# First attention of a two-layer network on one core: the loop over head pairs covers pairs 0 to 5, and the next batch's preparation sits at other places

## What is computed

```python
x = x + _L0_xattn_ref(_layernorm(x), ctx_768, w_q, w_kv, w_out, b_out)
# in it, per batch: 16 heads of 64 columns
q = query @ w_q;  k, v = jnp.split(context @ w_kv, 2, axis=-1)
scores = jnp.einsum('bhqd,bhkd->bhqk', q, k) * SCALE     # 512 x 1024 a head
attn = jax.nn.softmax(scores, axis=-1)
out = jnp.einsum('bhqk,bhkd->bhqd', attn, v)
return out @ w_out + b_out
```

## Time and profile before

| | us |
|---|---|
| median of three runs | 3585.0 (3582.49 to 3587.99) |
| profiled execution | 3589.58 |
| its span | 3587.8 |
| TensorE busy with matmuls | 3279.4 (91%) |
| VectorE, ScalarE, GpSimd busy | 2358.0, 1675.5, 1287.6 |
| first attention, by its first and last exponential | 74.1 to 2027.7 (starts) |

### The profile page before, as it was taken

The page is one execution under the profiler, slowest core; times in us unless marked ns, Lnnn a source line. Parts: engine busy times, 40 slices in busy tenths (PEclk is TensorE's granted clock), DMA queues, the critical chain, the costliest instruction groups (busy, mean ns, idle before and its releaser), DMA issues. The chain is left out here.

```text
span 3587.8 us, 49338 instructions
## 1 busy us (share of the span) xinstructions
PE 3279.4 (91%) x14300; PEld 1899.6 (53%) x14300; DVE 2358.0 (66%) x3762; ACT 1675.5 (47%) x1904; POOL 1287.6 (36%) x609
## 2 busy tenths in 40 slices
PE   4999999999999999999999877899999999999576
PEld 3556556556555565565565444455555555554366
DVE  3664665665656647656646333778777877877699
ACT  2442443443443434434434322456566566566376
POOL 0674664764755647646646523000000000000101
PEclk8999999999999999999999988899999999999698
DMA  6543554554554544436445132343343343442202
GB/s 159 137 114 106 137 123 116 122 122 120 128 131 102 137 114 119 116 103 149 111 113 134 47 121 80 81 103 95 89 101 91 91 103 87 97 105 72 66 15 79
DMA packets 265159, 380.01 MB, mean 106 GB/s; under 512 B 35944, under 2 KB 170672, under 8 KB 265008
## 3 DMA queue, kind: packets, MB, share of 16 engines
q1 hardware_dynamic: 265008, 378.06, 42.4%
HBM read 82.22 MB, written 27.26 MB: 31 GB/s over the span
## 5 line engine op out<-in xcount | busy, mean ns | idle before, releaser
L863 POOL TENSOR_TENSOR a_prob_sum<-a_prob_sum,a_prob 128x1024 f32<-128x1024 f32 x384 | 918.1, 2391 | 131.5 <-ACT a_prob L582 106.8
L582 ACT ACTIVATE a_prob<-a_t 128x1024 f32<-128x1024 f32 x512 | 519.6, 1025 | 796.1 <-PE a_t L428 788.6
L1617 DVE TENSOR_REDUCE a_mhalves<-a_m 128x1 f32<-128x512 f32 x1024 | 689.9, 688 | 188.6 <-PE a_m L1368 184.2
L728 DVE TENSOR_REDUCE a_mhalves<-a_m 128x1 f32<-128x512 f32 x1024 | 688.2, 690 | 171.2 <-PE a_m L392 167.4
L1529 ACT ACTIVATE a_prob<-a_t 128x1024 f32<-128x1024 f32 x512 | 498.7, 1023 | 145.5 <-PE a_t L1388 140.7
L435 PE MATMUL a_o<-a_prob,a_v_pair 128*64 128x512 f32 x2048 | 497.2, 607 | 0.7 <-DMA a_v_pair<-a_v_all 0.7
L1368 PE MATMUL a_m<-a_vh,a_qz 128*128 128x512 f32 x1024 | 464.3, 464 | 36.1 <-DVE a_mhalves L1617 18.8
L392 PE MATMUL a_m<-a_kh_n,a_qz 128*128 128x512 f32 x1024 | 413.8, 435 | 43.0 <-DVE a_mhalves L728 28.6
L863 POOL TENSOR_TENSOR a_prob_sum<-a_prob 128x1024 f32<-128x1024 f32 x64 | 151.6, 2369 | 637.7 <-ACT a_prob L582 637.7
L420 PE MATMUL a_t<-a_q_hl,a_k_hh 128*128 128x512 f32 x1024 | 340.1, 414 | 29.9 <-issue 28.7
L1368 PEld LDWEIGHTS a_m<-a_vh,a_qz 128*128 128x128 f32 x1024 | 190.3, 189 | 325.1 <-DVE a_mhalves L1617 246.5
(11 more groups left out here) (242 smaller groups left out, 4090.9 us busy)
## 6 DMA issues: line engine op xcount, KB each, us to landing
a_k_hh<-a_kh_n SPq DMA_DIRECT2D x256, 256.0 KB, 4.5
a_k_lm<-a_kl_n SPq DMA_DIRECT2D x128, 256.0 KB, 4.9
a_v_pair<-a_v_all SPq DMA_DIRECT2D x64, 512.0 KB, 5.3
a_vs<-a_vh SPq DMA_DIRECT2D x256, 128.0 KB, 2.3
a_wk<-wk_parts SPq DMA_DIRECT2D x64, 256.0 KB, 2.8
a_q_hl<-a_qz SPq DMA_DIRECT2D x128, 128.0 KB, 2.3
a_q_hm<-a_qz SPq DMA_DIRECT2D x128, 128.0 KB, 2.4
a_q_hl<-a_ql_n SPq DMA_DIRECT2D x128, 128.0 KB, 2.4
```

Of the source, the lines that this page charges most:

```text
L582: nc.scalar.activation(prob[:, t % RING], ps_t[t % 2][:, :, :], ACT.Exp, scale=SCALE0).then_inc(s_exp, 1)
L728: nc.vector.tensor_reduce(mhalves[:, qt, hd, n:n + 1], ps_m[:, n, :], AX.X, ALU.max).then_inc(s_max, 1)
L863: nc.gpsimd.tensor_tensor(acc, prob[:, (t - 1) % RING] if t == 1 else acc, prob[:, t % RING], ALU.add).then_inc(s_acc, 1)
L1617: nc.vector.tensor_reduce(mhalfs[:, u, qt, h, k:k + 1], ps_m[:, k, :], AX.X, ALU.max).then_inc(s_max, 1)
```

## The change

- TensorE and ScalarE: the inner loop takes pairs 0 to 5 (three turns of two, `pair_in_six`). The separate code for pairs 0 and 5 is gone. TensorE's wait for the batch's values moves from the head of the batch to its end.
- TensorE: `turn_queries` moves in pair 6 from between the scores of tiles 0 and 1 to behind `max_rows`; the wait for ScalarE's copy moves in front of `project_q`. ScalarE copies the turned queries behind the kept row maxima, and splits the high context behind exponentials 4 and 6.
- VectorE: the statistics move behind the maxima of pair 1 (in pair 0's time), the scaling behind the maxima of pair 6 (in pair 5's time), the low context behind all maxima of its pair. GpSimd's power moves behind its seven additions of pair 0.
- SyncE: the stack of pair 1 moves behind the first two loads of values; the next context is loaded behind the stack and the values of pair 6.
- Start: the values of batch 0 are projected before ScalarE's copy of the turned queries is waited for.

```diff
+def pair_in_six(b, h, u):
+    return Pair(b, 2 * h + u, h + u // 2, u % 2)
...
@@ SyncE @@
                     sp.wait_ge(s_qk, KT * nx.g - KT)
+                elif loading is not None:
+                    sp.wait_ge(s_kq, 3 * loading.g - 3)
...
                 load_values(pair(b, 1))
+                stack(pair(b, 1), pair(b, 2))
                 if not first:
                     store(b - 1)
...
-                if not last:
-                    sp.wait_ge(s_ln, 14 * (b + 2))
-                    load_context(b + 1)
                 with sp.Fori(0, NP // 2 - 2) as h:
...
                 load_values(pair(b, NP - 2))
+                if not last:
+                    sp.wait_ge(s_ln, 14 * (b + 2))
+                    load_context(b + 1)
                 stack(pair(b, NP - 1), None if last else pair(b + 1, 0))
...
                     stack(pair(b + 1, 0), pair(b + 1, 1))
-                    stack(pair(b + 1, 1), pair(b + 1, 2))
...
@@ TensorE @@
                 scores(pr, 0)
-                if turned is not None:
-                    pe.wait_ge(s_lo, 3 * nx.g + 3)
-                    turn_queries(turned)
                 scores(pr, 1)
-                if turned is not None:
-                    pe.wait_ge(s_xnT, turned + 1)
...
                 if nx is not None:
                     max_rows(nx)
+                if turned is not None:
+                    turn_queries(turned)
                 probs_v(pr, 4)
                 probs_v(pr, 5)
                 if nn is not None:
+                    if turned is not None:
+                        pe.wait_ge(s_xnT, turned + 1)
                     project_q(nn)
...
             def batch(b, last):
-                pe.wait_ge(s_va, KT // 2 * (b + 1))
-                pe.wait_ge(s_vd, KT // 2 * (b + 1))
-                attend(pair(b, 0), pair(b, 1), pair(b, 2))
-                with pe.Fori(0, NP // 2 - 2) as h:
+                with pe.Fori(0, NP // 2 - 1) as h:
                     for u in range(2):
-                        attend(pair_in_loop(b, h, u), pair_in_loop(b, h, u + 1), pair_in_loop(b, h, u + 2))
-                attend(pair(b, NP - 3), pair(b, NP - 2), pair(b, NP - 1))
+                        attend(pair_in_six(b, h, u), pair_in_six(b, h, u + 1), pair_in_six(b, h, u + 2))
...
                 project_out(b)
+                if not last:
+                    pe.wait_ge(s_va, KT // 2 * (b + 2))
+                    pe.wait_ge(s_vd, KT // 2 * (b + 2))
...
             turn_queries(0)
-            pe.wait_ge(s_xnT, 1)
             pe.wait_ge(s_cl, 2)
+            pe.wait_ge(s_wh, 3)
             pe.wait_ge(s_wl, 2)
...
                 if t == KT // 2 - 1:
+                    pe.wait_ge(s_xnT, 1)
                     project_q(first)
...
@@ ScalarE @@
                     exps(pr, t)
-                    if turned is not None:
-                        if t == 0:
-                            keep_turned(turned)
-                        if t in (2, 4):
...
+                    if turned is not None and t in (4, 6):
...
+                        split_context_high(turned, t // 6)
                 if nx is not None:
                     keep_max_rows(nx)
+                if turned is not None:
+                    keep_turned(turned)
...
@@ VectorE @@
-                if normalised is not None:
-                    row_statistics(nc, dve, rows, stats, mv, veps[:], s_ln, 14 * normalised)
...
-                        if split is not None and c in (6, 12):
-                            split_context_low(split, c // 12)
                         take_max(nx, c)
                     join_max(nx)
...
+                if split is not None:
+                    split_context_low(split, 0)
+                    split_context_low(split, 1)
+                if measured is not None:
+                    dve.wait_ge(s_xin, 16 * measured)
+                    row_statistics(nc, dve, rows, stats, mv, veps[:], s_ln, 14 * measured)
+                if scaled is not None:
+                    scale_rows(nc, dve, rows, mv, rstd, xn, s_rstd, scaled + 1, s_ln)
                 if nn is not None:
                     split_low(nn)
...
-                attend(None, pair(b, 1), pair(b, 2), normalised=None if last else b + 1)
+                attend(None, pair(b, 1), pair(b, 2), measured=None if last else b + 1)
...
-                attend(pair(b, NP - 4), pair(b, NP - 2), pair(b, NP - 1))
+                attend(pair(b, NP - 4), pair(b, NP - 2), pair(b, NP - 1), scaled=None if last else b + 1)
...
@@ GpSimd @@
-                add_probs(b * NP, None if last else b + 1)
+                add_probs(b * NP)
+                if not last:
+                    rstd_of(b + 1)
```

More of the change, by code:

```diff
@@ L341, in _ @@
             stack(pair(0, 0))
-            load_w(pair(0, 2), 2)
-            stack(pair(0, 1))
             batch(0, True, False)
@@ L570, in _ @@
             pe.wait_ge(s_sel, 4)
+            pe.wait_ge(s_va, KT // 2)
+            pe.wait_ge(s_vd, KT // 2)
             with pe.Fori(0, B - 1) as b:
@@ L622, in attend @@
                     exps(pr, t)
-                    if turned is not None:
-                        if t == 0:
-                            keep_turned(turned)
-                        if t in (2, 4):
[L627 to L632, removed]
+                    if turned is not None and t in (4, 6):
+                        if t == 4:
+                            act.wait_ge(s_kq, 3 * NP * turned)
+                            act.wait_ge(s_cs, 48 * turned)
+                        split_context_high(turned, t // 6)
                 if nx is not None:
                     keep_max_rows(nx)
+                if turned is not None:
+                    keep_turned(turned)
                 if nn is not None:
@@ L648, in batch @@
             def batch(b, last):
-                attend(pair(b, 0), pair(b, 1), pair(b, 2))
-                with act.Fori(0, NP // 2 - 2) as h:
+                with act.Fori(0, NP // 2 - 1) as h:
                     for u in range(2):
-                        attend(pair_in_loop(b, h, u), pair_in_loop(b, h, u + 1), pair_in_loop(b, h, u + 2))
-                attend(pair(b, NP - 3), pair(b, NP - 2), pair(b, NP - 1))
+                        attend(pair_in_six(b, h, u), pair_in_six(b, h, u + 1), pair_in_six(b, h, u + 2))
                 if last:
@@ L744, in invert, with attend @@
                 nc.vector.reciprocal(recip[:, cols], ps_x[:, cols]).then_inc(s_rec, 1)
-            def attend(before, nx, nn, split=None, normalised=None):
-                if normalised is not None:
-                    row_statistics(nc, dve, rows, stats, mv, veps[:], s_ln, 14 * normalised)
+            def attend(before, nx, nn, split=None, measured=None, scaled=None):
                 if before is not None:
@@ L762, in attend @@
                     invert(before, 3)
-                if normalised is not None:
-                    scale_rows(nc, dve, rows, mv, rstd, xn, s_rstd, normalised + 1, s_ln)
+                if split is not None:
[6 more added lines that the diff above has]
+                    scale_rows(nc, dve, rows, mv, rstd, xn, s_rstd, scaled + 1, s_ln)
                 if nn is not None:
@@ L773, in batch @@
             def batch(b, last):
-                if not last:
-                    dve.wait_ge(s_tr, b + 1)
-                    dve.wait_ge(s_xin, 16 * (b + 1))
-                attend(None, pair(b, 1), pair(b, 2), normalised=None if last else b + 1)
+                attend(None, pair(b, 1), pair(b, 2), measured=None if last else b + 1)
                 with dve.Fori(0, NP // 2 - 2) as h:
@@ L848, in normalise, with add_probs @@
                                         o_raw[:], recip[:], ALU.mult).then_inc(s_ot, 1)
-            def add_probs(g, normalised=None):
+            def add_probs(g):
                 acc = prob_sum[:]
                 for t in range(1, KT):
-                    if t == 3 and normalised is not None:
-                        rstd_of(normalised)
                     pool.wait_ge(s_exp, KT * g + t + 1)
```

## The result

| | before | after |
|---|---|---|
| median, us | 3586.19 (3582.49 to 3587.99) | 3538.03 (3533.70 to 3539.58) |
| profiled execution; its span | 3589.58; 3587.8 | 3538.93; 3537.1 |

The ratio is 0.9865, 95% interval 0.9853 to 0.9876: 48 us faster, against 60.5 forecast. The time lies in the range (3512 to 3548), 13.5 above the predicted 3524.5.

What follows compares the result with a forecast made beforehand. TensorE was taken as the bound, busy 240.6 of 250.6 us in a batch. The terms -34 - 17.4 - 9.5 + 0.5 = -60.5 took 3589.6 to 3529.1 profiled, 3524.5 as median; range 3512 to 3548.

Steps and rivals of the forecast that it cites:

- first batch: Pair 0 of batch 0: statistics behind VectorE's maxima end the wait for x, 44.00 to 26.6 us: -17.4.
- pair 6: Moving TensorE's turn of the queries behind the row maxima costs +2.0 us in place of +3.35, seven times: -9.5.
- seams with their pair 0: Where TensorE's outer loop jumps back, 5.7 us gained at each of six seams by the shorter loop: -34.
- That the length decides: TensorE's outer branch reloads code at 1526 matmuls and weight loads; 1116 would stay held, like the second attention's 1312.
- rival A: VectorE's code load shows at the seam: 6 x 2.4 = 14 us back, 3539, chance 0.10.
- the first load stays just covered: VectorE at the seam: its code comes after 2.69 us, its first maximum is due after 2.74; cost taken 0.
- Rival B: TensorE's long outer branch stays because only two 16 KB pieces of code are kept: 3559, chance 0.10.
- SyncE's term of 0: Moving pair 1's stack behind the value loads, and the context load later, costs nothing: each comes before it is needed.
- the overlap of transposes and copy: In pair 6 TensorE's transposes run while it waits for ScalarE's split (1.03 us) and copy (1.00) before project_q.
- Rivals C and D: Inner branch loads code, 3650, chance 0.02; context late or ScalarE 3 us dearer in pair 6, 3545, chance 0.05.
- Start: Before batch 0, values projected ahead of the wait for the turned queries' copy: +0.5 us, bounds -2.8 and +4.
- The bridge to the median: Whole kernel: profiled execution taken as 4.6 us above the timed median, so 3529.1 becomes 3524.5.

Runs made afterwards that it cites:

- long_loop: The changed kernel with TensorE's old loop (pair 0, pairs 1 to 4 in the inner loop, pair 5 written out): 3573.06 us, ratio 0.9959.
- hint_before: The kernel before the change plus a branch prefetch hint on TensorE's outer loop, its length untouched: 3586.06 us, ratio 0.9993.
- loops_alone: The kernel before with only TensorE's and ScalarE's loops over pairs 0 to 5 and TensorE's wait for the values changed: 3586.01 us, ratio 0.9995.
- stats_front: The changed kernel with VectorE's statistics back in front of the maxima, SyncE's new order kept: 3574.53 us, run once.

## Why the prediction was right, and where its working was wrong

In sign and size the three terms came: first batch -17.3 (forecast -17.4), pair 6 7 x 1.47 = -10.3 (-9.5), seams with their pair 0 -26.6 (-34). Between the two profiled executions the span fell by 50.7 where the sum said 60.5.

- **Seam, 7.6 short.** The reload of code was the cause, and it is gone at 1116 matmuls and loads. That the length decides is half right: long_loop brings the load back, but hint_before keeps the full 1526 and loads nothing. And of the 4.8 us of each "issue" wait some 0.8 weren't the load: the seam without a jump has a wait of 0.83 too. The seam became 59.71 where 58.86 + 0.5 = 59.36 was taken (6 x 0.35 = 2.1). The bigger part is pair 0: 27.01 instead of 26.10 (6 x 0.91 = 5.5). This is rival A, smaller than its price of 14. The step that failed is "the first load stays just covered", which took 2.69 us for VectorE's load from a seam where the stack's transfers weren't moved yet. The stack, moved by the same change, was costed by when it is needed, and not by what would run beside it; it made the load 4.1 to 5.1.
- **Rival B** is out: 0.21 us and no piece of queue 8. The two kept pieces in that section of the Trainium skill (Runtime: NRT & Kernel Launch, Instruction fetch mechanics) don't describe TensorE here. The same section also gives TensorE room for 2048 instructions. The prediction left that out. hint_before agrees with it: the loop of 1526 matmuls and loads, some 1740 recorded instructions, goes round with no piece of queue 8. But without the hint the same loop reloads nine pieces, so room isn't all that counts. Where exactly the bound is no run shows.
- **First batch.** Size right, cause half told. The prediction gave all 17.4 to the statistics and 0 to SyncE's queue. The statistics' place alone gives 0.04 (42.45 to 42.41), the queue's order alone 10.4 (42.45 to 32.02), both together 15.7; the other 1.6 came with neither. The step that failed is SyncE's term of 0. The prediction followed what ended the wait (x at 87.16) and didn't ask what would end it next. Of two waits that lie one over the other, the profile shows only the later.
- **Pair 6.** Size right, on the wrong edit. Pair 6 is 1.87 over a plain one where 2.0 was taken, half of it (0.93) the wait for the copy. But the gain was booked on the turn and on the overlap of transposes and copy. Alone the turn gives 0.01, and 0.26 as the full change has it. VectorE's low halves, named there only as what would delay no maximum any more, give 1.21 without it and 2.14 with it.
- **Rivals C and D** didn't come: 24 inner branches at 0.24 at most; no wait on the context, though ScalarE's late splits cost 0.7 a batch.
- **Start.** +1.15 in these two traces, but the first exponential stood anywhere from 70.97 to 75.76 in the fourteen profiled kernels, of which nothing can be read. The last seam grew by 0.5 and the rest by 1.6, both unforecast and left open.
- **The bridge to the median.** The sum was shifted by the 4.6 us that before's profiled execution lay above its median. After's lay 0.9 above its own. That is 3.7 of the 13.5; the other 9.8 are the terms above.

What the terms hid is that they are no sum. The short branch alone is worth 0 (loops_alone, hint_before), and 35 in the company of the other edits (long_loop). Before the change TensorE and VectorE each reloaded code at the seam, at the same time. The prediction gave the clock back with the branch; in loops_alone the wait for VectorE took the clock down again, for 3.4 to 6.8 us at each jump. That the seams' terms came near the forecast needed the statistics' move, which has no term of its own at these seams: with them in front, pair 0 is 5.9 longer (stats_front).

## What to carry to other kernels

Where two engines stand still at the same jump, price removing one stall by what the other then shows, and check with the one edit alone. Behind every wait that a move is to remove, look for the next transfer or engine that would end it a little earlier, and give the gain to all the moves that it needs. A transfer that is moved costs not only by when it is needed: a burst at a loop's jump slows the loading of code. And after a hint on one loop, look at the branches of the loops behind it.

## What was not expected of the hardware

- A branch prefetch hint at the loop's head takes the backward branch from 3.7 to 0.24 us on TensorE, and VectorE's restart from 4.1 to 5.1 down to 0.3. It doesn't load the code earlier: the pieces are gone (queue 8 from 61 to 7, queue 14 from 40 to 10, between 60 and 1850 us).
- A load of code beside full transfer engines took 4.9 us on TensorE (3.7 otherwise) and 4.1 to 5.1 on VectorE (2.8 to 3.1).
- Whether an unedited loop reloads its code can change with instructions ahead of it: VectorE's in the second attention went from 0.28 to 3.85 us a jump after one hint was put in front, 18.2 us in all.
